# Attention in a fused two-layer kernel: row maximum and exponential issued two query tiles ahead, rotary work a step later

## What is computed

```python
qs, ksem = x @ wq_sem, x @ wk_sem              # 64 columns a head
qg, kg   = rope(x @ wq_geo), rope(x @ wk_geo)  # 64 columns a head, rotated
v        = x @ wv                              # 128 columns a head
scores   = g * qs·ksem / 8 + (1 - g) * qg·kg / 8
attn     = softmax(where(causal, scores, -1e9))
out      = (attn @ v) @ wo
```

## Time and profile before

| | |
|---|---|
| median of three runs | 1935.2 us (1932.26 to 1939.66) |
| the profiled execution's own time | 1957.88 us |
| its span | 1956.3 us |
| PE / DVE / ACT / POOL busy | 90% / 58% / 52% / 41% |
| mean granted clock of PE | 0.958 |
| attention loop, from the first transpose at 447 us to its end at 1503 us | about 1056 us |

### The profile page before, as it was taken

One profiled execution on the slowest core, in us unless ns is written; L12 is line 12 of the kernel. 1 busy time (PEld: TensorE's weight loads), 2 busy tenths in 40 slices (PEclk: granted clock), 3 DMA queues, 4 the chain that ended last, 5 costly groups with the idle time before them and its releaser, 6 DMA issues. The chain is left out here.

```text
span 1956.3 us, 34013 instructions
## 1 busy us (share of the span) xinstructions
PE 1752.7 (90%) x9530; PEld 1375.0 (70%) x9530; DVE 1136.6 (58%) x2173; ACT 1026.0 (52%) x2244; POOL 803.0 (41%) x788
## 2 busy tenths in 40 slices
PE   6399989338999999999999999999997999999998
PEld 2255656327878888788788788888886766666777
DVE  4799953695665565655555555556563333333567
ACT  4599923015656566666666565656564334443322
POOL 1489931423344444344434343444441233212354
PEclk9699999568999999999999999999999999999989
DMA  4742348200000000000000000000103999999623
GB/s 138 291 182 102 102 149 268 88 0 17 20 20 7 25 14 11 19 17 22 14 11 19 19 6 24 14 24 8 41 6 99 284 308 310 304 308 300 180 88 96
DMA packets 100409, 193.36 MB, mean 99 GB/s; under 512 B 15460, under 2 KB 59748, under 8 KB 97748
## 3 DMA queue, kind: packets, MB, share of 16 engines
q1 hardware_dynamic: 58836, 108.76, 18.2%
q0 software_dynamic: 17152, 47.67, 7.7%
q10 hardware_dynamic: 24336, 35.98, 5.6%
HBM read 140.84 MB, written 51.51 MB: 98 GB/s over the span
## 5 line engine op out<-in xcount | busy, mean ns | idle before, releaser
L1196 POOL TENSOR_TENSOR sw<-sw,rope_t 64x512 f32<-64x512 f32 x128 | 164.1, 1282 | 594.3 <-ACT sw L1006 594.3
L916 PE MATMUL ps<-pt,v 128*128 128x256 f32 (+1 forms) x1280 | 278.8, 365 | 8.1 <-DVE v L1085 7.1
L998 ACT ACTIVATE pb<-ps,negmax 128x128 f32<-128x128 f32 (+7 forms) x256 | 190.6, 744 | 146.7 <-DVE negmax L1069 146.6
L916 PEld LDWEIGHTS ps<-pt,v 128*128 128x128 f32 x1280 | 234.1, 191 | 37.2 <-issue 7.1
L985 ACT COPY pt<-ps 128x512 f32<-128x512 f32 (+3 forms) x384 | 171.3, 481 | 83.7 <-PE ps L906 70.3
L906 PE MATMUL ps<-ident,pb 128*128 128x128 f32 x1152 | 173.0, 277 | 46.1 <-ACT pb L998 44.9
L550 POOL DMA_DIRECT2D w2r<-in_w x148 | 77.2, 522 | 333.2 <-PE ps L599 289.3
L1199 POOL TENSOR_TENSOR t<-t,sw 64x512 f32<-64x512 f32 x128 | 185.7, 1451 | 32.7 <-POOL sw L1196 16.0
L906 PEld LDWEIGHTS ps<-ident,pb 128*128 128x128 f32 x1152 | 132.4, 141 | 85.6 <-ACT pb L998 33.1
L1069 DVE TENSOR_REDUCE negmax<-ps 128x1 f32<-128x128 f32 (+7 forms) x256 | 191.4, 748 | 0.0
L633 DVE SCALAR_TENSOR_TENSOR ga<-th,ps 128x176 f32<-128x176 f32 x148 | 50.0, 338 | 241.3 <-ACT th L614 241.3
(11 more groups left out here) (206 smaller groups left out, 4055.7 us busy)
## 6 DMA issues: line engine op xcount, KB each, us to landing
w13r<-in_w SPq DMA_DIRECT2D x124, 352.0 KB, 6.5
w2r<-in_w POOLq DMA_DIRECT2D x148, 176.0 KB, 6.5
result<-yy ACTq DMA_DIRECT2D x148, 128.0 KB, 5.5
crow<-c_rows SPq DMA_DIRECT2D x32, 512.0 KB, 3.6
t<-sorted SPq DMA_DIRECT2D x124, 128.0 KB, 5.8
sorted<-zeros ACTq DMA_DIRECT2D x15, 1024.0 KB, 17.0
hc<-in_w SPq DMA_DIRECT2D x24, 352.0 KB, 6.0
wraw<-in_wqk SPq DMA_DIRECT2D x16, 256.0 KB, 2.7
```

What stands on the lines that cost most here:

```text
L916: last = pe.matmul(ps[:, 6, c0:2 * P], v[:, j, hd], pt[g % 2][:, j, c0:2 * P], start=j == 0, stop=j == 2 * g + 1)
L998: act.activation(pb[:, qt % 2, 0:cols], ps[:, bank:bank + 2, :].rearrange("p a n -> p (a n)")[:, 0:cols], ACT.Exp, bias=negmax[:, par, qn: ...
L1196: g.tensor_tensor(sw[64:128, p % 2, :], sw[64:128, p % 2, :], rope_t[64:128, 1, (p // 2) * 512:(p // 2 + 1) * 512], ALU.mult).then_inc(s_t ...
```

## The change

Four things in the three functions `att_pe`, `att_act` and `att_dve`:

- ACT and DVE take the exponential and the maximum of tile `qt + 2` in step `qt`, not of tile `qt + 1`; those of tile 1 of the very first head are put ahead of the loop.
- The second heads' steps make their pieces (of the next first head) in steps 1, 2, 3 and 5, the first heads' in 2, 3, 5 and 6 as before.
- `swap` and `turned` of a piece stand in the step after its matmuls, behind `probs` on ACT and ahead of `max_tile` on DVE. `rounded` and `rest` stand two steps after the matmuls, behind the exponential and the maximum of that step. For the first head's last piece that is step 0 of the next iteration.
- `add_out` of the projections of steps 3, 5, 7 and 1 stands at the head of steps 4, 6, 0 and 2.

```diff
-        PIECE = {2: 0, 3: 1, 5: 2, 6: 3}
+        PIECE = ({2: 0, 3: 1, 5: 2, 6: 3}, {1: 0, 2: 1, 3: 2, 5: 3})
+        def piece_at(hh, qt):
+            return PIECE[hh].get(qt)
...
-                    if qt in PIECE and not last:
-                        p = PIECE[qt]
-                        if qt == 2 and next_b == 0:
+                    if qt in PIECE[hh] and not last:
+                        p = PIECE[hh][qt]
+                        if p == 0 and next_b == 0:
...
             exp_tile(0, 0, 0)
+            exp_tile(0, 1, 0)
...
                     probs(it, qt)
-                    if qt < 7 or not last:
-                        exp_tile(it, qt + 1, hh)
+                    swapped = piece_at(hh, qt - 1)
+                    if swapped is not None and not last:
+                        swap(n0 + swapped, swapped, piece_fill(pair, hh, swapped))
                     if qt == 0 and not first(it):
                         output(it - 1, 3)
                     if qt in (2, 4, 6):
                         output(it, qt // 2 - 1)
-                    if qt in PIECE and not last:
-                        p = PIECE[qt]
-                        swap(n0 + p, p, piece_fill(pair, hh, p))
-                    if qt in (3, 4, 6, 7) and not last:
-                        p = {3: 0, 4: 1, 6: 2, 7: 3}[qt]
-                        rounded(n0 + p, p, 1 - hh)
+                    if qt < 6 or not last:
+                        exp_tile(it, qt + 2, hh)
+                    turned_before = piece_at(hh, qt - 2)
+                    if turned_before is not None and not last:
+                        rounded(n0 + turned_before, turned_before, 1 - hh)
+                    if qt == 0 and hh == 1:
+                        rounded(4 * it + 3, 3, 1)
...
             max_tile(0, 0, 0)
+            max_tile(0, 1, 0)
...
-                    if qt < 7 or not last:
-                        max_tile(it, qt + 1, hh)
                     if qt == 0 and not first(it):
-                        rest(n0 - 1, 3, hh)
-                    if qt in (4, 5, 7) and not last:
-                        p = {4: 0, 5: 1, 7: 2}[qt]
-                        rest(n0 + p, p, 1 - hh)
+                        add_out(it - 1, 2, prev_b, 1 - hh)
+                    if qt == 2 and not first(it):
+                        add_out(it - 1, 3, prev_b, 1 - hh)
+                    if qt in (4, 6):
+                        add_out(it, qt // 2 - 2, b, hh)
+                    turning = piece_at(hh, qt - 1)
+                    if turning is not None and not last:
+                        turned(n0 + turning, turning)
+                    if qt < 6 or not last:
+                        max_tile(it, qt + 2, hh)
                     if qt == 0 and not first(it):
                         output(it - 1, 3)
-                    if qt == 1 and not first(it):
-                        add_out(it - 1, 3, prev_b, 1 - hh)
                     if qt in (2, 4, 6):
                         output(it, qt // 2 - 1)
                     if qt in (3, 7):
                         invert(it, qt // 7, hh)
-                    if qt in (3, 5, 7):
-                        add_out(it, qt // 2 - 1, b, hh)
+                    resting = piece_at(hh, qt - 2)
+                    if resting is not None and not last:
+                        rest(n0 + resting, resting, 1 - hh)
+                    if qt == 0 and hh == 1:
+                        rest(4 * it + 3, 3, 1)
                     if qt in VALUE and hh == 0:
                         values(VALUE[qt], value_fill(pair, VALUE[qt]))
-                    if qt in PIECE and not last:
-                        p = PIECE[qt]
-                        turned(n0 + p, p)
...
+            add_out(ITS - 1, 2, 1, 1)
             output(ITS - 1, 3)
             add_out(ITS - 1, 3, 1, 1)
```

## The result

The changed kernel takes 2133.91 us (median of four runs, 2131.13 to 2136.14) beside 1937.43 us for the kernel before (also a median of four): ratio 1.1013, 95% interval 1.0977 to 1.1049. It is slower, as forecast, but by 196 us and not by 135, and it lies outside the range that ended at 2120.

A forecast was written before the change was run, and what follows sets the result against it. PE was taken to bound the attention. New waits of 12.2 us a pair against 3.85 gave +8.35, times 16 pairs +134; splits +10, first and last iterations -9: 1935.2 + 135 = 2070 us, range 2010 to 2120.

The forecast's parts named there:

- Bank 7 after a piece: PE waits for `turned` behind the later swap: three waits of 0.84 us and one of 1.5 a pair.
- Bank 6 in step 0: `output` waits for the moved `add_out` of group 2: 1.6 us behind a second head, 0.8 behind a first.
- lateness: Delay handed on from one chain to the next across PE, ACT and DVE queues: some 2.5 us a pair.
- the 0.4 us beside POOL: First head's `rest` of piece 2 slowed beside POOL's work: 0.4 us a pair, 6 us, only in the high end.
- Bank 6 in step 6: `output` of group 2 waits for `add_out` of group 1 in both heads: 2 x 1.64 = 3.3 us a pair.
- The sum of the waits: New PE waits in attention: 12.2 us a pair, low end 9.7, against 3.85 before.
- the splits: Weight splits on DVE, coming between a value copy or `rest` and what PE waits for: 10 us in all taken.
- the first and the last group: First iteration lacks an addition to wait for (2.0 less), the last makes no piece (7 less): -9 us.
- the lower clock: Rival, 8%: PE's waits bring its 1.2 GHz level, three times a pair, 120 us more: 2190.
- The removed wait: PE's eight waits for the exponential in four iterations go: 6.5 us, about 52 us over 8 groups.
- Headroom: Weight-load share would leave PE 24.6 us in 132.60, at most 197 us to win; the prediction called most no waiting.

The follow-up runs named there:

- e3_swap_first: The changed kernel with `swap` ahead of `probs` on ACT in the same step: ratio 1.0538 to the kernel before.
- e4_exp_only: The kernel before with only maximum and exponential taken two tiles ahead: ratio 0.989 to the kernel before.
- e1_fill: The changed kernel with 8 more matmuls, results overwritten, ahead of the projections of groups 1 and 2: ratio 1.0887 to the kernel before.
- v5: Changed kernel: additions back, swap before `probs`, exponential before ACT's `output`, value copy before `rest`, first heads' piece 1 rounded early, splits in step 0, values before `output`: 0.9755.
- v4: Changed kernel: additions back, swap before `probs`, value copy before `rest`, all `rounded` and `rest` early, splits in step 0, first heads' values before `output`: ratio 1.023.

## Why the prediction was right and where it failed

**Which way.** Right. "What counts is what the new order of three in-order queues puts ahead of what PE waits for": the exponential left the list of waits and the three others took its place, as written.

**Bank 7 after a piece** (2.5 and 1.5 us a pair). Right. The three waits of 0.84 show as 0.70 to 0.81 us, with 0.16 more for the pipeline, and the one of 1.5 as 1.46. `e3_swap_first` removed them with one moved line.

**Bank 6 in step 0** (1.6 and 0.8). The chain behind a second head was right: 3.28 us against 3.20, a wait of 1.80. The one behind a first head was too small, 1.57 to 1.81 shown against 0.8, since the copy of values waits for more than its own matmuls. Timeline of DVE there, and of POOL:

```profile
634.48 1.08 DVE L1082 TENSOR_TENSOR qkl<-t,qkr 128x512 fp32r<-128x512 f32 x1 [1.13 <-ACT qkr L1014]
635.48 0.68 DVE L1092 COPY v<-ps 128x512 f32<-128x512 f32 x1
636.08 0.86 DVE L1104 SCALAR_TENSOR_TENSOR xr<-ps,rinv,xr 128x256 f32<-128x256 f32 x2
...
633.72 1.29 POOL L1210 TENSOR_TENSOR t<-t,sw 64x512 f32<-64x512 f32 x1 [0.16 <-POOL sw L1207]
```

`rest` ahead of it waits for `rounded` and then takes 1.08 us beside POOL. The sum had this under lateness and, for the 0.4 us beside POOL, only in its high end. It belonged in the middle.

**Bank 6 in step 6** (1.64 each). Right for the second head, 1.68, and 2.36 in iterations with a split; in the first head the scores of tile 8 take most of it, 1.49 or 0.87 to 0.95, as written.

**The sum of the waits.** Forecast were 12.2 us a pair, and with 10 / 8 for the splits 25.7 us in four iterations. In the four at full clock the table of waits, 516.46 to 669.02 us, has these:

```profile
PE ps L920 <- DVE xr L1104: 14.1, 11, 2.4
PE ps L860 <- DVE t L1088: 6.6, 7, 1.5
PE ps L860 <- DVE qkl L1082: 2.4, 2, 1.5
PE ps L920 <- DVE v L1092: 1.6, 1, 1.6
```

24.7 us in 21 waits, and with 21 x 0.16 that makes 28.1. The group grew by 152.56 - 132.60 = 19.96 us where the terms taken come to 2 x 8.35 + 10 / 8 = 17.95. Over eight groups that is 16 us of the miss. In the first and the last group the growth at full clock was 17.6 and 17.3 us, together 5 us below two of the others, where 9 had been taken off: 4 more. The other groups are up to 0.7 us longer at full clock than the one added up here. At full clock the change costs 157 us and not 135. By itself this would not have left the range: 1937 + 157 = 2094.

**What failed: the clock.** "With a wait of 1.37 us in every pair the clock was 1.00 throughout" was the ground for putting the lower clock at 8% and at nothing in the forecast. The waits grew to 1.8 and 2.4 us, 21 in four iterations in place of ten, and the trace of before had no row for such waits inside the loop; I carried a row over beyond where it was measured. The length of the longest wait doesn't decide by itself either: `e4_exp_only`, whose waits inside the loop are at most 1.04 us, has two stretches at half clock, behind waits of 0.94 and 0.57 us close together, and the kernel before has none with 1.4. The rival's mechanism was right (PE's waits bring the lower level: with work in them 6 stretches are left of 23, `e1_fill`) and its size was off: 39 us, not 120, because 23 stretches came and not the 48 that three waits in each of 16 pairs would bring, and one costs 39.1 / 23 = 1.7 us, not 2.5. Which waits bring one stays open. It should have been a term of the sum with ends at 0 and 120, and not a separate case; the range would then have held 2134.

**The removed wait.** The 52 us are not there for the taking either: alone, the earlier exponential gives 12 to 21 (`e4_exp_only`), and most of the 7.7 us a group come free only in v5, which gains 132.6 - 126.0 = 6.6.

**Headroom.** By the Trainium skill ("Perfetto Trace Analysis", on the most-contended engine) the share of weight loads is a measure of headroom. In v5, where PE waits for nearly nothing, it is 865.94 of 1002 us, 86%. So the rows decide that 86 to 88% is this kernel's ceiling, and that of the 19% which this measure seemed to leave in the earlier trace rows some 5 were waits.

## What to carry to other kernels

Where queues run in order, don't ask only what a moved instruction waits for, but what stands behind it on its queue and who needs that: additions of 0.9 us each, put behind a rounding behind an exponential, cost 86 us in all, and putting them back in their places saved them. Find for each single buffer the chain from its last fill to its next, add it up from rows, and compare it with what the bound engine does in between; the chains of this case came out within 0.2 us where the queue was free at their start. Move only what is on such a chain: taking all roundings early made new waits of 2 us, taking one of them early removed a wait of 0.9.

## What the runs showed of the hardware that I had not expected

PE's granted clock fell to its 1.2 GHz level inside a busy loop in which no wait is longer than 2.4 us and PE is busy for 81 to 85% of an iteration at full clock, 23 times in 1250 us and at the same cost in two executions; in the kernel before, with waits up to 1.4 us, not once after the start; in `e4_exp_only`, with waits up to 1.04 us, twice. Useless matmuls in the waits brought it back (23 stretches to 6) and made the kernel faster, by 1.2% in the ratios and 0.7% in the profiled attention.

A `rest` on DVE, two operands in SBUF, took 0.68 us alone, 1.08 in the changed kernel beside POOL's rotation and 1.71 in v4, where POOL had started just before it:

```profile
890.60 1.28 POOL L1209 TENSOR_TENSOR t<-t,sw 64x512 f32<-64x512 f32 x1 [0.16 <-POOL sw L1206]
```

In these three `rest` ends 0.55 or 0.56 us after POOL's operation: 875.91 after 875.36 in the kernel before, 635.56 after 635.01, 892.44 after 891.88. In the kernels before and after, 56 of 256 start while one of POOL's long operations runs, and all 56 end like this; the other 200 take 0.7 us. This agrees with the Trainium skill ("SBUF — State Buffer", the rules for kernel authors), by which the second of two such operations is blocked until the first ends. The 0.4 us that the prediction took from the earlier trace rows was not a third of that rule's effect but what it comes to when `rest` starts 0.76 us after POOL.
